# A decoder layer on one core: attention outputs divided on packed rows that DMAs lay, instead of on token rows that TensorE turns

## The chip, the core and the metric

The kernel runs on one core of a Trainium2 chip. The core has TensorE (PE: matrix products and transposes, results in PSUM), VectorE (DVE), ScalarE (ACT), GpSimd (POOL) and SyncE (SP), which here only issues DMAs. Each engine runs its own instructions in order and waits on semaphores for the others. The metric is the device time of one execution in microseconds.

## The reference

A decoder layer in fp32 on 16 sequences of 256 tokens, width 256, 16 heads of 16: causal self-attention, cross-attention to a context, and a mixture of 8 experts with 2 chosen per token, each with a residual and a layer norm.

```python
k, q, v = x @ Wk.T, x @ Wq.T, x @ Wv.T          # per head; k and q normalised per head
att = softmax(where(causal, -inf, q k^T))        # 16 heads, 256 x 256 each
x = layernorm(x + (att @ v) @ Wo.T + bo)
Q, K, V = x @ Wq + bq, ctx @ Wk + bk, ctx @ Wv + bv   # rotary positions on Q and K
x = layernorm(x + (softmax(Q K^T / 4) @ V) @ Wo + bo)
x = layernorm(x + moe(x))                        # top 2 of 8 experts, 256 -> 512 -> 256
```

## The kernel before

Attention runs first, then the experts. Attention is 32 blocks: block n below 16 is the self-attention of sequence n, block n from 16 up the cross-attention of sequence n - 16. A block has 16 heads in 4 groups of 4. The work is a software pipeline of quarters: in quarter q each engine runs the steps whose place in the pipeline falls on it (`q = 4 n + AT`), in an order written out by hand at the end of each engine's part, by r = q mod 4. Each quarter carries the scores of one group (`score`, lines 494 to 510), the maxima of an earlier step's scores (`maxima`, L1075, on VectorE, a first and a second half), the transposed scores (`score_T`, L534), their exponentials (`weights`, L871, ScalarE), and the weighted sum of a group (`weigh`, L555). Four such quarters are one block.

`weigh` multiplies by `vaug`, in which each head has 16 columns of values and 16 columns of ones. So its result for a group, 128 x 256, holds for each of the 4 heads 16 rows of outputs and below them 16 equal rows of the sum of the weights, tokens along the free axis. ScalarE copies it to `oT` (`drain_pv`, L882). What follows for block n:

- quarter r = 2 (`OUT_AT` = 18): TensorE turns `oT` to token rows, four transposes for each half of the tokens (`turn_o`, L655). VectorE inverts the 16 sums per token (L1204, 128 x 16) and multiplies (L1208, 128 x 256), once for each half (`divide`).
- quarter r = 3 (`PROJECT_AT` = 19): TensorE turns the result back (`turn_on`, L669, four transposes) before `weigh`, ScalarE copies it (`drain_onT`, L854), and at the end of the quarter, behind `score_T` and the transposes of the next keys (`turn_qk("k01")`, L645), TensorE multiplies by the output weights (`project_o`, L681). VectorE adds the residual (`residual`, L1219) at the end of its quarter, behind maxima, `combine` (L1082) and `variances` (L1152).

All small results of TensorE (everything but the scores) go through a ring of two PSUM slots. `ring_places` lists the jobs in TensorE's order; a job may start when the one two places before it is drained. `k01` is drained by ScalarE (L920), and the scores of quarter r = 0 wait for that copy.

SyncE issues the DMAs in order. In quarter r = 0: the maxima rows to their place (`lay_max`, L382, four DMAs) and, for 12 of the blocks (n = 2 to 13), two DMAs of 1.5 MB each that fill the experts' row buffer in HBM with padding rows (`lay_pads`, L392; one more of 1.1 MB at n = 2, L395). In r = 1, in self-attention, the next rows of x (`load_xb`, L375); in r = 3 the next transposed inputs (`load_xin`, L367).

## Time and profile before

| | |
|---|---|
| time, median of 3 runs | 1244.41 us (1242.04 to 1250.48) |
| the profiled execution, its own time | 1243.51 us |
| its span in the profile | 1241.8 us |
| TensorE / VectorE / ScalarE / GpSimd busy | 88% / 65% / 46% / 22% |
| mean granted TensorE clock | 0.926 of full speed |
| period of a self-attention block | 22.4 us |
| period of a cross-attention block | 25.6 to 28.6 us at full clock |

Attention takes the first 900 us of the span, the experts the rest. The granted clock is 1.00 (2.4 GHz) or 0.50 (1.2 GHz) at any moment; a number between is a mean over a stretch. In the rows of a stretch an engine's number is its busy time in us. A row of the order of time merges neighbours of one kind; "[1.82 <-PE PS L510]" behind it says that the engine had been idle for 1.82 us until that line of TensorE released it.

### The profile page before, as it was taken

Reading aid. Unit: us, or ns where it says so; the run is one execution under the profiler, and the core shown is the slowest. Engines: PE = TensorE matmul, PEld = TensorE weight load, DVE = VectorE, ACT = ScalarE, POOL = GpSimd, SP = SyncE. Lnnn points to the kernel's source line nnn. Section 1 sums busy time; section 2 is a strip of 40 time slices with the busy share of each in tenths; the row PEclk is TensorE's granted clock in tenths of the full one; section 3 lists DMA queues with packets and bytes.
Section 4 is the critical chain, followed back from the end, with each engine's and each line's share of the span. In section 5 each row is a group of like instructions: output and inputs, shape, how many; then the busy total and the mean of one; then the engine's idle time right before and its main releaser. Section 6 shows DMA issues by size and latency. Waiting matters only on the chain.

```text
span 1241.8 us, 29875 instructions
## 1 busy us (share of the span) xinstructions
PE 1096.5 (88%) x11181; PEld 801.0 (65%) x11181; DVE 801.8 (65%) x1935; ACT 575.2 (46%) x937; POOL 274.3 (22%) x311
## 2 busy tenths in 40 slices
PE   5899999999999899999999999888539999999920
PEld 3456666666666666666666666555439999999920
DVE  5647777778788787687777786753624444444447
ACT  2356666666655555555455554544212222222214
POOL 4022223232222200003030302202132222222210
PEclk9889999999999999999899998876669999999975
DMA  6104644635531000101010100001057767777654
GB/s 229 63 22 160 203 150 143 201 126 183 169 118 29 10 11 19 44 10 48 10 46 11 47 15 33 29 11 38 22 173 209 211 220 213 212 220 214 194 235 188
DMA packets 94651, 139.31 MB, mean 112 GB/s; under 512 B 11216, under 2 KB 68944, under 8 KB 93104
## 3 DMA queue, kind: packets, MB, share of 16 engines
q1 hardware_dynamic: 87888, 114.98, 29.8%
q0 software_dynamic: 6624, 22.42, 4.7%
q8 instruction: 93, 1.52, 0.5%
q14 instruction: 46, 0.38, 0.1%
HBM read 76.56 MB, written 60.29 MB: 110 GB/s over the span
## 4 chain that ended last, share of the span: by engine, by line
PE 75%; DVE 14%; issue 5%; ACT 3%; DMA 2%; POOL 1%; SPq 1%; ACTq 0%; POOLq 0%; DVEq 0%
PE PS L792 10%; PE PS L803 10%; PE PS L534 9%; PE PS L555 8%; PE PS L645 5%; PE PS L503 5%; PE PS L614 4%; PE PS L610 4%; DVE part L1075 3%; PE PS L681 3%; PE PS L628 2%; PE PS L510 2%; PE PS L655 2%; PE PS L669 2%; PE PS L506 2%
## 5 line engine op out<-in xcount | busy, mean ns | idle before, releaser
L1075 DVE TENSOR_REDUCE part<-PS 128x6 f32<-128x768 f32 (+1 forms) x256 | 272.5, 1087 | 114.2 <-PE PS L510 65.2
L871 ACT ACTIVATE pT<-PS 128x768 f32<-128x768 f32 (+1 forms) x256 | 220.8, 914 | 96.7 <-PE PS L534 96.7
L1536 POOL TENSOR_SCALAR_AFFINE_SELECT pT<-pT 128x512 f32<-128x512 f32 x128 | 87.6, 689 | 294.2 <-ACT pT L871 291.2
L534 PE MATMUL PS<-big 17*128 17x256 f32 (+1 forms) x2048 | 142.0, 393 | 9.7 <-DVE part L1075 6.6
L792 PEld LDWEIGHTS PS<-oT,big 128*128 128x128 f32 x1136 | 139.3, 194 | 5.2 <-ACT oT L982 1.6
L555 PE MATMUL PS<-pT,vaug 128*32 128x256 f32 (+1 forms) x2048 | 130.9, 375 | 12.0 <-DVE sq L1178 4.6
L792 PE MATMUL PS<-oT,big 128*128 128x128 f32 x1136 | 139.9, 277 | 1.0 <-ACT oT L982 1.0
L534 PEld LDWEIGHTS PS<-big 17*128 17x128 f32 x2048 | 98.7, 194 | 57.7 <-DVE part L1075 28.2
L803 PE MATMUL PS<-w2s,qkn 128*128 x568 | 134.4, 380 | 0.0
L1553 POOL DMA_INDIRECT xs_dram<-rows_all,posi x64 | 64.3, 1004 | 298.8 <-DVE posi L1331 282.9
L982 ACT ACTIVATE oT<-PS 128x256 f32<-128x256 f32 x71 | 27.2, 383 | 192.5 <-PE PS L781 192.5
L1572 POOL DMA_INDIRECT p_dram<-pT,rowid x71 | 68.1, 959 | 209.7 <-DVE rowid L1433 202.4
L803 PEld LDWEIGHTS PS<-w2s,qkn 128*128 128x128 f32 x568 | 102.4, 190 | 11.3 <-issue 0.3
L555 PEld LDWEIGHTS PS<-pT,vaug 128*32 128x32 f32 x2048 | 57.2, 112 | 60.3 <-issue 35.3
L882 ACT ACTIVATE oT<-PS 128x256 f32<-128x256 f32 x128 | 49.0, 383 | 98.9 <-PE PS L555 98.4
L1417 DVE TENSOR_TENSOR qkn<-PS,b1T 128x512 f32<-128x512 f32 x71 | 49.1, 691 | 65.2 <-PE PS L792 65.2
L645 PE MATMUL PS<-ident,big 128*128 128x128 f32 x512 | 84.5, 289 | 6.7 <-DVE on L1208 4.2
L1427 DVE TENSOR_TENSOR pT<-PS,w_self 128x256 f32<-128x256 f32 x71 | 30.1, 424 | 87.8 <-PE PS L803 87.8
L503 PE MATMUL PS<-big 16*128 16x256 f32 x1024 | 76.3, 413 | 9.4 <-ACT big L916 6.1
L645 PEld LDWEIGHTS PS<-ident,big 128*128 128x128 f32 x512 | 55.0, 143 | 42.7 <-issue 32.3
L614 PE MATMUL PS<-w_self,xin 128*128 128x512 f32 x128 | 68.4, 664 | 1.7 <-DVE w_self L1017 1.3
L503 PEld LDWEIGHTS PS<-big 16*128 16x128 f32 x1024 | 48.0, 190 | 27.4 <-ACT big L916 11.9
(166 smaller groups left out, 1603.6 us busy)
## 6 DMA issues: line engine op xcount, KB each, us to landing
big<-w SPq DMA_DIRECT2D x71, 512.0 KB
xs_dram<-zrow SPq DMA_DIRECT2D x24, 1496.0 KB, 9.0
oT<-xs_dram SPq DMA_DIRECT2D x71, 136.0 KB, 3.5
xin<-xT SPq DMA_DIRECT2D x16, 256.0 KB, 2.8
w2s<-w POOLq DMA_DIRECT2D x1, 4096.0 KB, 12.9
xb<-x SPq DMA_DIRECT2D x16, 256.0 KB, 10.6
xin<-ctxT SPq DMA_DIRECT2D x16, 256.0 KB, 2.8
big<-p_dram SPq DMA_DIRECT2D x4, 1024.0 KB, 7.9
```

Source lines behind the costliest of these rows:

```text
L503: ins = pe.matmul(o, q, a[r0:r0 + D, 1, g, :], start=True, stop=True)
L534: ins = pe.matmul(o, keys, a[r0:r1, 0, g, q0:T], start=True, stop=True)
L555: ins = pe.matmul(o[PADDED * i:PADDED * (i + 1), q0:T], vaug[:, n % 4, kt, GRP * g + i, :], pT[:, k % 2, i, kt * T:kt * T + T - q0], start ...
L614: ins = pe.matmul(o, a[:, c, t * P:(t + 1) * P], w_qk[:, c, :], start=(c == 0), stop=(c == KC - 1))
L645: ins = pe.transpose(ring_slot(job)[:, j * T + t * P:j * T + (t + 1) * P], src, ident[:])
L792: ins = pe.matmul(moe_bank(1, j % 2)[:, f * P:(f + 1) * P], w1s[:, j % W1_BUFFERS, c, f * P:(f + 1) * P], xsT[:, j % 2, c * P:(c + 1) * P] ...
L803: ins = pe.matmul(moe_bank(3, j % 2)[:, 0:E], hact[:, j % 2, c * P:(c + 1) * P], w, start=(c == 0), stop=(c == FC - 1))
L871: act.activation(pT[:, k % 2, 2 * half:2 * half + 2, 0:wide], src, ACT.Exp).then_inc((exp_a, exp_b)[half], 1)
L1075: dve.tensor_reduce(dst, src, AX.X, ALU.max, negate=True).then_inc((max_a, max_b)[half], 1)
L1536: pool.affine_select(d, d, [[0, 2], [0, 2], [1, P]], ALU.is_ge, 0.0, base=0, channel_multiplier=-1).then_inc(masked, 1)
L1553: pool.indirect_dma_start(out=xs_dram, out_offset=bass.IndirectOffsetOnAxis(ap=posi[:, batch_index(last), c:c + 1], axis=0), in_=rows_all[ ...
L1572: pool.indirect_dma_start(out=p_dram, out_offset=bass.IndirectOffsetOnAxis(ap=rowid[:, o, 0:1], axis=0), in_=ye[:, o], in_offset=None).the ...
```

## The change

The two turns on TensorE go, and the copy between them. `oT` is laid on packed rows by SyncE: `packed` has 128 partitions (16 per head, 8 heads in one slice of the free axis and 8 in the other), once for the outputs and once for the sums. 16 DMAs per block move 16 rows x 2 groups x 256 tokens each (32 KB), 8 for groups 0 and 2 in quarter r = 0 (`PACK_AT` = 16), 8 for groups 1 and 3 in quarter r = 1. VectorE inverts all 128 x 512 sums and multiplies 128 x 512 once per block, at the end of quarter r = 2. `project_o` reads `packed` and moves from the end of quarter r = 3 to its start, ahead of `weigh`, so the ring's order there is `wo`, `pv`, `k01`. Per block the change takes away 12 transposes, one copy on ScalarE, and two inversions and two products on VectorE; it adds 16 DMAs, one inversion and one product.

```diff
@@ ring_places, in the order of quarters
-            place("o0", block_at(q, OUT_AT))
-        else:
-            place("onT", block_at(q, PROJECT_AT))
+        elif r == 3:
+            place("wo", block_at(q, PROJECT_AT))
         place("pv", group_at(q, WEIGH_AT))
@@ SyncE
+            def pack(n, b):
+                if n is None:
+                    return
+                if b == 0 and n >= 1:
+                    await_filled(sp, ("wo", n - 1))
+                for g in range(b, NG, 2):
+                    await_drained(sp, ("pv", (n, g)))
+                for k in range(2):
+                    for i in range(GRP):
+                        r0, r1 = PADDED * i + D * k, (GRP * b + i) * D
+                        sp.dma_start(packed[r1:r1 + D, k], oT[r0:r0 + D, n % 2, b::2, :]
+                                     ).then_inc(packed_in[n % 2], 16)
@@
                 load_xb(block_at(q, MAXT_AT + 1))
+                pack(block_at(q, PACK_AT), 0)
+                pack(block_at(q, PACK_AT + 1), 1)
                 n = block_at(q, MAXT_AT)
                 if n is not None:
                     lay_pads(n)
@@ TensorE
             def project_o(n):
-                await_drained(pe, ("onT", n))
+                pe.wait_ge(divided, n + 1)
-                        ins = pe.matmul(ring_slot(job)[:, t * E:(t + 1) * E], onT[:, c, t * P:(t + 1) * P],
+                        ins = pe.matmul(ring_slot(job)[:, t * E:(t + 1) * E], packed[:, 0, c, t * P:(t + 1) * P],
@@
-                    turn_o(block_at(q, OUT_AT), 0)
-                else:
-                    turn_on(block_at(q, PROJECT_AT))
+                elif r == 3:
+                    project_o(block_at(q, PROJECT_AT))
                 weigh(group_at(q, WEIGH_AT))
@@
-                    turn_o(block_at(q, OUT_AT), 1)
@@
                     turn_qk("k01", block_at(q, TURN_K01), 1, 0)
-                    project_o(block_at(q, PROJECT_AT))
@@ ScalarE
-                    await_filled(act, ("o1", n - 2))
+                    act.wait_ge(packed_in[n % 2], 256 * (n // 2))
@@
-                elif r == 3:
-                    drain_onT(block_at(q, PROJECT_AT))
@@ VectorE
+            def divide(n):
+                dve.wait_ge(packed_in[n % 2], 256 * (n // 2 + 1))
+                dve.reciprocal(packed[:, 1], packed[:, 1]).then_inc(inverted, 1)
+                dve.wait_ge(inverted, n + 1)
+                dve.tensor_tensor(packed[:, 0], packed[:, 0], packed[:, 1], ALU.mult).then_inc(divided, 1)
@@
                     maxima(group_at(q, SCORE_AT), 0)
-                    divide(block_at(q, OUT_AT), 0)
                     maxima(group_at(q, SCORE_AT), 1)
                     scale_heads(block_at(q, SCALE_AT))
                     lay_out(block_at(q, LAY_AT))
-                    divide(block_at(q, OUT_AT), 1)
+                    divide(block_at(q, PROJECT_AT - 1))
```

The change moves lines by a few numbers; in the rows below `project_o` is L681 before and L668 of the changed kernel, `score_T` L534 and L545, `weigh` L555 and L566, `turn_qk` L645 and L656. On TensorE, from the scores of a quarter r = 3 to those of the next r = 0 in self-attention, before:

```order
L506 MATMUL PS<-big 128x128 x4
L510 MATMUL PS<-big 128x256 x4
L669 MATMUL PS<-ident,on 128x128 x4
L555 MATMUL PS<-pT,vaug 32x256 x4
L555 MATMUL PS<-pT,vaug 32x128 x4
L534 MATMUL PS<-big 128x256 x4
L534 MATMUL PS<-big 128x128 x4
L645 MATMUL PS<-ident,big 128x128 x4
L681 MATMUL PS<-w_self,onT 128x256 x4
```

And in the changed kernel:

```order
L517 MATMUL PS<-big 128x128 x4
L521 MATMUL PS<-big 128x256 x4
L668 MATMUL PS<-w_self,packed 128x256 x4
L566 MATMUL PS<-pT,vaug 32x256 x4
L566 MATMUL PS<-pT,vaug 32x128 x4
L545 MATMUL PS<-big 128x256 x4
L545 MATMUL PS<-big 128x128 x4
L656 MATMUL PS<-ident,big 128x128 x4
```

The output projection stands where the four transposes stood, and the transposes of the keys are now the last thing before the next scores.

On SyncE, from the maxima rows of one block to the next transposed input, in a block that fills padding, before:

```order
L367 DMA xin<-xT 128x2x256
L382 DMA big<-nmaxT 1x4x256 x4
L392 DMA xs_dram<-zrow 128x11x272 x2
L375 DMA xb<-x 128x2x256
L367 DMA xin<-xT 128x2x256
```

And in the changed kernel (`xin` is L363 there, `nmaxT` L378, `zrow` L401, `xb` L371):

```order
L363 DMA xin<-xT 128x2x256
L378 DMA big<-nmaxT 1x4x256 x4
L391 DMA packed<-oT 16x2x256 x8
L401 DMA xs_dram<-zrow 128x11x272 x2
L371 DMA xb<-x 128x2x256
L391 DMA packed<-oT 16x2x256 x8
L363 DMA xin<-xT 128x2x256
```

The first eight new DMAs stand ahead of the padding, the second eight behind the padding and the rows of x.

## Rows read from the trace of the kernel before

**Rows 1.** The page: busy us by engine and share; a DMA issue, KB, us to landing.

```profile
PE 1096.5 (88%) x11181; PEld 801.0 (65%) x11181; DVE 801.8 (65%) x1935; ACT 575.2 (46%) x937; POOL 274.3 (22%) x311
...
xin<-xT SPq DMA_DIRECT2D x16, 256.0 KB, 2.8
```

**Rows 2.** The chain in order of time, 200 to 260 us: start, us, engine and line.

```profile
221.59 0.59 PE PS L655 x4
...
227.68 0.59 PE PS L669 x4
228.27 0.79 PE PS L555 x16
229.05 0.87 PE PS L534 x16
...
230.50 1.73 PE PS L681 x8
...
232.26 0.30 PE PS L494 x16
```

**Rows 3.** VectorE in order of time, 221 to 233 us: start, us, line, operation.

```profile
221.67 0.96 DVE L1075 TENSOR_REDUCE part<-PS 128x6 f32<-128x768 f32 x1 [1.12 <-PE PS L510]
...
224.03 1.28 DVE L1141 TENSOR_TENSOR big<-qkn,chain 128x512 f32<-128x512 f32 x2
...
227.76 1.82 DVE L1075 TENSOR_REDUCE part<-PS 128x6 f32<-128x768 f32 x2 [1.82 <-PE PS L510]
...
229.80 1.22 DVE L1152 TENSOR_REDUCE vv<-sq 128x64 f32<-128x1024 f32 x1
232.27 0.69 DVE L1219 TENSOR_TENSOR y<-PS,xb 128x512 f32<-128x512 f32 x1 [1.26 <-PE PS L681]
```

**Rows 4.** ScalarE in order of time in the same block.

```profile
217.20 0.38 ACT L882 ACTIVATE oT<-PS 128x256 f32<-128x256 f32 x1
...
229.98 1.51 ACT L871 ACTIVATE pT<-PS 128x768 f32<-128x768 f32 x2 [0.48 <-PE PS L534]
231.38 0.78 ACT L920 ACTIVATE big<-PS,gv 128x512 f32<-128x512 f32 x1
```

**Rows 5.** Groups by line and shape, whole span: busy us, mean ns of one.

```profile
L1204 DVE RECIPROCAL rec<-PS 128x16 f32<-128x16 f32 x64 | 15.9, 248 | 17.8 <-PE PS L655 17.7
...
L1292 DVE RECIPROCAL prob<-odds 128x4 f32<-128x4 f32 x7 | 1.2, 178 | 0.2
```

**Rows 6.** SyncE's DMA issues in order of time, the same block.

```profile
211.62 2.47 SPq L382 DMA_DIRECT2D big<-nmaxT  x4
214.14 1.31 SPq L392 DMA_DIRECT2D xs_dram<-zrow  x2
215.49 3.61 SPq L375 DMA_DIRECT2D xb<-x  x1
226.18 0.38 SPq L367 DMA_DIRECT2D xin<-xT  x1
```

**Rows 7.** DMA issues, 214 to 232 us: KB each, us from issue to landing.

```profile
xb<-x SPq DMA_DIRECT2D x1, 256.0 KB, 11.3
```

**Rows 8.** Stretches: length, busy us of PE, PEld, DVE, ACT, POOL, PEclk, DMA share, GB/s.

```profile
613.70:644.60 30.90, 29.60 (x270) 19.80 (x270) 20.18 (x46) 15.12 (x23) 10.68 (x10) 0.89 0.14 46
...
672.90:700.70 27.80, 26.46 (x270) 18.13 (x270) 20.25 (x46) 15.12 (x23) 10.68 (x10) 1.00 0.15 52
...
426.00:427.00 1.00, 0.00 (x0) 0.00 (x0) 0.93 (x4) 0.57 (x1) 0.00 (x0) 1.00 0.00 0
...
430.00:431.00 1.00, 1.00 (x10) 0.36 (x3) 0.83 (x6) 0.24 (x1) 0.00 (x0) 0.50 0.00 0
```

**Rows 9.** VectorE in a cross-attention block: the pair of maxima of its quarter 3.

```profile
692.59 2.36 DVE L1075 TENSOR_REDUCE part<-PS 128x4 f32<-128x1024 f32 x2 [2.45 <-PE PS L503]
```

**Rows 10.** ScalarE in order of time, the last block, 876 to 882 us.

```profile
876.55 0.38 ACT L882 ACTIVATE oT<-PS 128x256 f32<-128x256 f32 x1 [1.23 <-PE PS L555]
...
881.05 0.60 ACT L854 ACTIVATE onT<-PS 128x512 f32<-128x512 f32 x1 [0.26 <-PE PS L669]
```

## What the change does to the time

> **What bounds the kernel now.** First the page: TensorE is busy for 1096.5 of some 1242 us [rows 1]. Then the chain of waits in order of time: through a self-attention block it runs over TensorE alone, and each group starts where the last one ended [rows 2]. So a microsecond taken off TensorE looks like one won, as long as the other engines have room for it. Two transposing steps of 0.59 us in quarter 2 (one stands in the rows) and one in quarter 3 [rows 2] are 1.77 us per block, 57 us over 32 blocks. Then the order of time on VectorE, ScalarE and SyncE in the same block, which says how much room there is: VectorE waits 1.12 us before quarter 2's maxima and 1.82 us before quarter 3's [rows 3]. ScalarE's copy of `k01` ends at 232.16, and the scores of the next quarter 0 start at 232.26 [rows 2, 4]: that copy is as late as it may be, and only because the 1.73 us of output projection lie between it and the scores.
>
> **The inversion.** It is the dearest new operation and no row shows its size. 128 x 4 takes 178 ns, 128 x 16 takes 248 ns [rows 5]: 5.8 ns per element and partition, where a product of 128 x 512 takes 0.69 us in all [rows 3]. At 5.8 ns, 508 further elements come to 2.96 us, so I take 3.14 us. The lower bound is the 0.69 us of the product. The upper bound scales the larger row, fixed part and all: 32 x 0.248 = 7.9 us; the two rows speak against that, since four times the elements cost 1.4 times as much.
>
> The Trainium skill (VectorE: DVE Perf Modes, First, the fixed hardware budget) says that the inversion is an iterative divide with a repeat count of 8. At 8 cycles of that page's kind per element, 0.96 GHz as Trainium Kernel Development and Optimization of the Trainium skill (NeuronCore Architecture) has it, it would be some 4.3 us, an estimate; the trace's 5.8 ns per element lies below it. By that estimate the sum below would be some 35 us larger.
>
> **A block whose DMAs come in time.** I walk one self-attention block, with the times of the rows as they stand.
> - VectorE, quarter 2: the first maxima start at 221.67 as before, the pair takes 1.82, `scale_heads` 1.28 [rows 3]: 224.8. Inversion and product 3.83: 228.65. Before, the two small inversions and products took 1.34 together.
> - TensorE does not gain quarter 2 in full. Without the first turn `weigh` ends at 222.4, but `score_T` waits for the first maxima (222.63 at the earliest), so 0.2 of 0.59 us is won there. The second 0.59 counts in full. The scores of quarter 3 end at about 226.8 instead of 227.68 (before, quarter 3's first transposes began there [rows 2]).
> - `project_o` is next and waits for the product: 228.65, 1.9 us idle. It takes 1.73, `weigh` 0.79, `score_T` 0.87 [rows 2]: 232.1. Behind the waiting projection stand all three, and the exponentials wait for them.
> - `k01` needs the ring slot of `wo`, which `residual` drains. VectorE does its pair of maxima (1.82, from 228.65), `combine` (0.17, about what a short operation takes), `variances` (1.22) and `residual` (0.69) [rows 3]: 232.6. So `k01` runs to 233.2.
> - ScalarE's exponentials end at 232.1 + 0.1 + 1.51 = 233.7, its copy of `k01` at 234.5 [rows 4]. The cover (the projection) is gone: the scores start at 234.55 instead of 232.26 [rows 2].
>
> That is +2.3 us per block instead of -1.77. Are the DMAs in time? Group 3 is copied at 217.20 + 0.38 [rows 4]. A DMA with the same number of dimensions takes SyncE 0.38 us, 0.41 with its gap; one of `lay_max` takes 0.61 [rows 6]; eight take 3.3 (bounds 3.0 to 4.9). Landing is 2.8 us after issue for `xin` [rows 1], so all is there at about 223.4, before 224.8. Hidden, with 1.4 us to spare; at 0.61 each it is just hidden.
>
> **Blocks with padding.** Here they are not in time. The two fills are issued at 214.14; the issue of `xb` behind them takes 3.61 us instead of the 0.38 of its like [rows 6], so the queue is full, and `xb` lands 11.3 us after it started, at 226.8 [rows 7]. The second eight DMAs stand behind both. The first eight stand ahead of the fills and wait for group 2's copy, so they push the fills back by 3.3 us: `xb` lands at 230.1, and the last packed rows, 256 KB more on the same queue, at about 230.7. VectorE is ready at 224.8: it waits 5.9 us, and everything of the walk above moves by that. +8.2 us per block. These are blocks 1 to 12 (the pack of block m shares a quarter with the fill of m + 1), 12 x 8.2 = 98 us; the third fill at n = 2 adds its 1.1 MB, at the rate of the others (3.25 MB in some 11 us) 3.5 us. Lower bound: if the queue did not hold them, 2.3 each.
>
> The Trainium skill (DMA: Bandwidth & Descriptors, Queues, rings and completion order) speaks against this change: each DMA engine takes the descriptors of one issuer's queue in ring order. The long issue of `xb` in the trace agrees with it. By that rule the padded blocks cost the 98 us; without it they would cost 28.
>
> **The clock.** TensorE would stand idle from 226.8 to about 234.6 in such a block. In the trace it stood idle through 426 to 427, and at 430 the granted clock was 0.50, that is 1.2 GHz [rows 8]. A block in which the clock fell took 30.9 us, a like one at full clock 27.8 [rows 8]: 3.1 us. 12 blocks x 3.1 = 37 us. Lower bound 0 (it doesn't fall), upper bound twice that (it stays low for twice as long).
>
> **The rest.** Blocks 0, 13, 14 and 15 have no fill beside them: 4 x 2.3 = 9 us. In cross-attention VectorE idled 2.45 us before quarter 3's pair [rows 9], and what it gets more there is 3.83 - 1.34 = 2.5 us, so that pair starts where it did. The logits' product still lies between `k01` and the next scores, so no cover is lost. What remains is `k01` waiting for the residual: 0.5 us by the same walk, and some 1.5 in every second block, where the router's choice stands behind the division. 14 x 1.0 = 14 us; bounds -1 and +2.5 per block. At the end nothing hides the DMAs: in the last block group 3 is copied at 876.93 and the projection could start at 881.65 [rows 10]. Now 3.3 + 2.4 for issue and landing and 3.83 on VectorE: 886.5, 4.8 later; 3 more in the block before. 8 us.
>
> **Sum.** 98 + 3.5 + 37 + 9 + 14 + 8 = 169.5 us on the profiled execution's own 1243.5 us: 1413 us. That execution is 0.9 us under the median of the runs, so nothing is added.
>
> **Rivals.**
> - *The queue does not hold the packed rows* (they land as in other blocks, and the clock stays). 12 x 2.3 instead of 12 x 11.3 + 3.5: 1413 - 112 = 1301. For it: only two DMA types are seen behind a fill, and one of them has no late user. Against: 11.3 us for 256 KB.
> - *The inversion is cheap* (0.69 us, the lower bound). 2.45 us less in 12 blocks, 1.9 in 4 and some 1.5 in 14, where other waits take over: 58 us less, 1355. Against it: the slope in rows 5.
> - *All of it dearer*: inversion half as long again (4.7 us), or the clock low for twice as long, or falling in cross-attention too, where a fall cost 3.1 us: 1413 + some 60 = 1475.
> - *Faster: TensorE's sum decides.* If the divided rows lay ready when quarter 3's scores end, nothing of the walk waited for the projection, and 57 us of transposes went: 1187. It decides from the point where inversion and product together take less than 226.8 - 224.8 = 2.0 us and the rows have landed by 224.8, in padded blocks too. Even then the copy of `k01` has lost its cover. 3 in 100.
> - *No change*: the gain in some blocks balances the stall in others, which takes a cheap inversion and early landing both. 3 in 100.
>
> **Numbers.** The forecast has 52 in 100 (its own range 1365 to 1455), the dearer case 18, the queue that doesn't hold 15, the cheap inversion 9, no change 3, faster 3. The range 1300 to 1490 leaves out some of the dearer case and of the first rival, and the last two. A measurement of this kernel can tell about 1% from no change. Slower by over 1%: 0.94, within 1%: 0.03, faster by over 1%: 0.03.
>
> **What would show it.** In the changed profile: one inversion of 128 x 512 per block with its mean (3.1 us right; 0.7 or 4.7 wrong). Idle time of VectorE before it, released by the DMAs, about 6 us in 12 blocks and none in the others. Idle time of TensorE before the projection. Block periods of about 34 us up to 500 us of the span, then 24 to 29. A clock below 1.00 in self-attention. Idle of TensorE before quarter 0's scores, released by ScalarE's copy of `k01`. It would be wrong if the packed rows landed early beside the fills, or if the issue of one took much more than 0.4 us: at 1 us each even the free blocks would wait.

## The result, and the profile after

The changed kernel takes 1509.15 us (median of 4 runs, 1504.82 to 1512.9) against 1243.22 us of the kernel before on the same chip: ratio 1.212, interval 1.208 to 1.216. The forecast was 1413 us, in a range of 1300 to 1490. The direction was right, and the loss is half as large again as forecast: 269 us between the two profiled executions instead of 169.5.

| | before | after |
|---|---|---|
| span in the profile, us | 1241.8 | 1511.1 |
| TensorE busy, us | 1096.5 | 1170.1 |
| VectorE busy, us | 801.8 | 878.9 |
| mean granted TensorE clock | 0.926 | 0.819 |
| one of the 12 blocks with padding, maxima rows to maxima rows, us | 22.4 to 24.5 | 36.9 to 41.3 |
| a cross-attention block, us | 25.6 to 31.5 | 29.6 to 35.8 |

TensorE has 12 transposes per block less and is busy for longer, because the same products run at the lower clock. First the page: an engine's busy time; then the costliest groups (busy us, mean ns of one, idle time before them and its releaser) and the DMA issues (KB each, median us to landing).

```profile
PE 1170.1 (77%) x10797; PEld 822.1 (54%) x10797; DVE 878.9 (58%) x1871; ACT 555.0 (37%) x905; POOL 269.0 (18%) x311
...
L1173 DVE RECIPROCAL packed<-packed 128x512 f32<-128x512 f32 x32 | 107.2, 3349 | 117.9 <-DMA packed<-oT 117.9
...
packed<-oT SPq DMA_DIRECT2D x512, 32.0 KB, 2.0
```

The inversion takes 3.35 us, and VectorE stood idle for 117.9 us ahead of it, always for the packed rows. Next the waits of TensorE: total, times, longest.

```profile
PE PS L668 <- DVE packed L1175: 146.4, 28, 11.5
PE PS L505 <- ACT big L893: 24.4, 14, 1.8
PE PS L514 <- ACT big L889: 20.3, 26, 2.0
```

The projection (L668) waits for the division, and the scores (L505 in self-attention, L514 in cross-attention) for ScalarE's copy of `k01`: the two waits of the walk. A block with padding in order of time: SyncE's issues, then VectorE, TensorE and ScalarE. They answer to [rows 6], [rows 3], [rows 2] and [rows 4].

```profile
259.37 2.55 SPq L378 DMA_DIRECT2D big<-nmaxT  x4
262.03 5.16 SPq L391 DMA_DIRECT2D packed<-oT  x8
267.23 1.39 SPq L401 DMA_DIRECT2D xs_dram<-zrow  x2
268.67 4.27 SPq L371 DMA_DIRECT2D xb<-x  x1
273.04 8.00 SPq L391 DMA_DIRECT2D packed<-oT  x8
...
282.44 3.35 DVE L1173 RECIPROCAL packed<-packed 128x512 f32<-128x512 f32 x1 [6.55 <-DMA packed<-oT]
285.82 0.69 DVE L1175 TENSOR_TENSOR packed<-packed 128x512 f32<-128x512 f32 x1
...
286.57 3.78 PE L668 MATMUL PS<-w_self,packed 128*128 128x256 f32 x8 [8.43 <-DVE packed L1175]
...
294.54 0.40 PE L505 MATMUL PS<-identb,strips 32*128 32x64 bf16 x16 [1.76 <-ACT big L893]
...
293.66 0.78 ACT L893 ACTIVATE big<-PS,gv 128x512 f32<-128x512 f32 x1
```

Eight packing DMAs take SyncE 5.16 us, 0.64 each, and the eight behind `xb` 8.00 us. VectorE gets the rows 23.07 us after the first DMA of the maxima rows (259.37 to 282.44); over the 12 blocks with padding it is 23.2 us on the mean, 26.1 in the one with the third fill and 22.4 to 23.7 in the others. The landings of `xb`, of the first packing DMA behind it and of the last two:

```profile
xb<-x SPq DMA_DIRECT2D x1, 256.0 KB, 11.3
...
packed<-oT SPq DMA_DIRECT2D x1, 32.0 KB, 5.8
...
packed<-oT SPq DMA_DIRECT2D x2, 32.0 KB, 2.0
```

The first one behind the padding takes 5.8 us from its issue to its landing. The last one takes 2.0, as the median of all 512 does, so the packed rows are complete 2.0 us after SyncE has begun the last issue: the padding delays them by holding up SyncE's issues. TensorE is then idle for 8.43 us, does the projection in 3.78 us instead of 1.73, and waits 1.76 us more for `k01`. Last, the stretches of attention (length, busy us of PE, PEld, DVE, ACT and POOL, clock, DMA share, GB/s): all of it and then the last 16 blocks, of after.

```profile
0.00:1102.40 1102.40, 866.95 (x8716) 548.80 (x8719) 689.43 (x1299) 447.95 (x702) 176.15 (x215) 0.81 0.26 75
...
593.60:1102.40 508.80, 445.50 (x4047) 290.67 (x4048) 372.82 (x750) 224.94 (x350) 68.28 (x66) 0.85 0.15 38
```

And of before, for the same blocks:

```profile
0.00:848.00 848.00, 793.33 (x9073) 525.15 (x9073) 617.88 (x1359) 466.99 (x732) 181.40 (x215) 0.96 0.24 78
...
394.30:848.00 453.70, 424.85 (x4235) 287.16 (x4233) 332.05 (x782) 235.69 (x366) 68.40 (x66) 0.95 0.08 24
```

Attention, up to the last maxima rows, grew by 254 us. TensorE's idle time in it went from 54.7 to 235.5 us: +181. Its busy time went up by 73.6 although 57 us of transposes are gone, so 130 us are the same work at the lower clock. 181 - 57 + 130 = 254. In the last 16 blocks it is +34 us of idle time, -28 of transposes, +49 of clock: +55.

### The profile page after: what moved, and what is told of

It reads as the page before. It is cut to its first block, busy times and chain, and to the rows that moved or that the text cites. A ratio compares the mean times of both kernels' runs of the same rounds, so it can differ in the third digit from the quotient of the medians.

```text
span 1511.1 us, 29429 instructions
## 1 busy us (share of the span) xinstructions
PE 1170.1 (77%) x10797; PEld 822.1 (54%) x10797; DVE 878.9 (58%) x1871; ACT 555.0 (37%) x905; POOL 269.0 (18%) x311
## 4 chain that ended last, share of the span: by engine, by line
PE 60%; DVE 17%; SPq 8%; issue 5%; ACT 5%; DMA 3%; POOL 1%; ACTq 0%; POOLq 0%; DVEq 0%
PE PS L775 9%; PE PS L786 8%; PE PS L545 8%; PE PS L566 7%; SPq L391 6%; DVE packed L1173 6%; PE PS L668 6%; PE PS L625 4%; PE PS L621 4%; PE PS L514 4%; DVE part L1046 3%; ACT pT L844 2%; PE PS L656 2%; DMA packed<-oT 2%; PE PS L521 2%
## 5 line engine op out<-in xcount | busy, mean ns | idle before, releaser
L1173 DVE RECIPROCAL packed<-packed 128x512 f32<-128x512 f32 x32 | 107.2, 3349 | 117.9 <-DMA packed<-oT 117.9
L545 PE MATMUL PS<-big 17*128 17x256 f32 (+1 forms) x2048 | 156.8, 427 | 20.1 <-DVE part L1046 18.8
L1501 POOL TENSOR_SCALAR_AFFINE_SELECT pT<-pT 128x512 f32<-128x512 f32 x128 | 81.8, 640 | 506.4 <-ACT pT L844 502.4
L566 PE MATMUL PS<-pT,vaug 128*32 128x256 f32 (+1 forms) x2048 | 155.0, 430 | 8.6 <-issue 5.3
L668 PE MATMUL PS<-w_self,packed 128*128 128x256 f32 x128 | 54.9, 603 | 125.8 <-DVE packed L1175 125.8
L545 PEld LDWEIGHTS PS<-big 17*128 17x128 f32 x2048 | 108.0, 215 | 79.6 <-issue 40.0
L668 PEld LDWEIGHTS PS<-w_self,packed 128*128 128x128 f32 x128 | 37.0, 303 | 139.7 <-DVE packed L1175 132.2
L566 PEld LDWEIGHTS PS<-pT,vaug 128*32 128x32 f32 x2048 | 62.0, 125 | 87.1 <-issue 64.7
L514 PE MATMUL PS<-big 16*128 16x256 f32 x1024 | 83.4, 444 | 23.1 <-ACT big L889 20.3
L656 PE MATMUL PS<-ident,big 128*128 128x128 f32 x512 | 84.2, 289 | 9.9 <-DVE y L1185 6.1
L625 PE MATMUL PS<-w_self,xin 128*128 128x512 f32 x128 | 84.9, 803 | 1.7 <-DVE w_self L988 1.3
```

Source lines behind the costliest of these rows:

```text
L514: ins = pe.matmul(o, q, a[r0:r0 + D, 1, g, :], start=True, stop=True)
L545: ins = pe.matmul(o, keys, a[r0:r1, 0, g, q0:T], start=True, stop=True)
L566: ins = pe.matmul(o[PADDED * i:PADDED * (i + 1), q0:T], vaug[:, n % 4, kt, GRP * g + i, :], pT[:, k % 2, i, kt * T:kt * T + T - q0], start ...
L625: ins = pe.matmul(o, a[:, c, t * P:(t + 1) * P], w_qk[:, c, :], start=(c == 0), stop=(c == KC - 1))
L656: ins = pe.transpose(ring_slot(job)[:, j * T + t * P:j * T + (t + 1) * P], src, ident[:])
L668: ins = pe.matmul(ring_slot(job)[:, t * E:(t + 1) * E], packed[:, 0, c, t * P:(t + 1) * P], w[:, c, :], start=(c == 0), stop=(c == KC - 1))
```

## Experiments

Ratios are to the kernel before on the same chip, with their 95% intervals. Unless said otherwise the edit is made to the changed kernel, which gave 1.211 again:

> The changed kernel itself once more, so that the runs beside it are compared on one chip. Every theory expects its ratio to the kernel before of 1.21 again.

Measured: 1.2111 (1.2069 to 1.2152).

Four runs need care: `pads_later`, `busy_wait`, `cheap_inverse` and `wo_last` ran on a chip on which the kernel before took 1269 us (1260 to 1277), 2% more than the 1240 to 1246 elsewhere, and the changed kernel did not run there. The intervals don't cover that. So their gains over the changed kernel are given twice, by the difference of the ratios and by that of the medians; which of the two is nearer is not known.

A second caution: the last 16 blocks (maxima rows to maxima rows) are the same program in the changed kernel, in `busy_self` and in `pads_later`. They took 508.5, 492.8 and 526.4 us, at clocks of 0.86, 0.89 and 0.84. The last two:

```profile
567.56:1060.35 492.79, 432.56 (x4056) 283.12 (x4059) 371.86 (x751) 224.68 (x349) 68.75 (x66) 0.89 0.15 39
...
508.12:1034.50 526.38, 455.12 (x4048) 296.47 (x4051) 373.49 (x751) 224.32 (x349) 66.94 (x66) 0.84 0.14 37
```

So kernels that differ only in the first half of attention differ by 16 to 18 us in the second, and the clock with it; what sets it there is not shown. A gain of that size is placed only by looking at the blocks themselves.

**The DMAs alone.** The kernel before, with `pack(...)` at its two places and no reader.

```diff
+                pack(block_at(q, OUT_AT - 2), 0)
+                pack(block_at(q, OUT_AT - 1), 1)
```

> The kernel before, unchanged in what it computes, with the 16 packing DMAs of each block added at the places that they have in the changed kernel; nothing reads the packed rows, and only the reuse of oT two blocks later waits for them. My theory: the DMAs cost through whoever waits for them and not by themselves. In a fill block xb then lands some 20.5 us after the first DMA of the maxima rows, which is 232.1 on the times of the kernel before, where the residual wants it at 232.3: ratio 1.000 to 1.010. Rival: the transfers or their issue disturb the rest (xin and xb late on SyncE's queue, traffic to SBUF): 1.03 or more, which would be a part of the 21% that does not come from the wait for the division.

Measured: 1.0074 (1.0031 to 1.0118). So 512 further DMAs cost under 1% by themselves. But SyncE has no room left in a block with padding:

```profile
193.23 2.55 SPq L384 DMA_DIRECT2D big<-nmaxT  x4
195.89 5.16 SPq L397 DMA_DIRECT2D packed<-oT  x8
201.09 1.40 SPq L407 DMA_DIRECT2D xs_dram<-zrow  x2
202.54 4.83 SPq L377 DMA_DIRECT2D xb<-x  x1
207.47 7.57 SPq L397 DMA_DIRECT2D packed<-oT  x8
215.09 0.58 SPq L369 DMA_DIRECT2D xin<-xT  x1
215.72 2.55 SPq L384 DMA_DIRECT2D big<-nmaxT  x4
```

From one block's maxima rows to the next (22.5 us) it issues without a pause. What costs is who waits for these DMAs.

**Padding behind the packed rows.**

```diff
-                n = block_at(q, MAXT_AT)
+                n = block_at(q, MAXT_AT + 1)
                 if n is not None:
                     lay_pads(n)
```

> The changed kernel with the two padding fills issued behind the second eight packing DMAs instead of ahead of them; nothing else moves. Queue theory: in the 12 blocks with a fill the packed rows land some 2 us after their last issue, VectorE's wait before the inversion (117.9 us in the changed kernel) falls below 20 us, and since TensorE's idle stretch of about 8 us there shrinks to about 2, the clock recovers too: 12 x (6.5 + some 5 us of half clock) = 140 us less, some 1370 us. Rival (the DMAs are late from their own 16 issues of 0.6 us, not from the fills): the wait stays and the time stays within 20 us of 1509.

Measured: 1.137 (1.128 to 1.146), 93 us less by the ratios and 63 by the medians, and not the 140 expected. The 12 blocks with padding take 371 us instead of 454, 29.7 to 31.7 each and one 34.0. VectorE's wait for the rows in them fell from 91 to 21 us. In six of them the rows are still late by 2.4 to 3.7 us, in the other six by under 0.5. One of the first six:

```profile
258.64 5.55 SPq L391 DMA_DIRECT2D packed<-oT  x8
264.24 0.58 SPq L371 DMA_DIRECT2D xb<-x  x1
264.94 6.08 SPq L391 DMA_DIRECT2D packed<-oT  x8
...
272.48 3.35 DVE L1174 RECIPROCAL packed<-packed 128x512 f32<-128x512 f32 x1 [3.45 <-DMA packed<-oT]
```

The maxima rows start at 255.96, VectorE is ready 13.1 us later, as the walk had it (224.8 - 211.6), and the rows are there after 16.5. In the walk they were there after 11.8. SyncE's last issue ends 15.1 us after the maxima rows started, where the block of the changed kernel above has 21.7: the 6.6 us between them are the whole difference of the landings (16.5 for 23.1).

**The first eight from GpSimd's queue.** In the changed kernel (`after_pool`), and with the padding and the projection moved as well (`pool_queue`).

```diff
-                pack(block_at(q, PACK_AT), 0)
...
+                        pool.dma_start(packed[r1:r1 + D, k], oT[r0:r0 + D, n % 2, 0::2, :]
+                                       ).then_inc(packed_lo[n % 2], 16)
```

> The changed kernel with one edit: GpSimd issues the first eight packing DMAs of each block, so that the padding on SyncE's queue starts 5.2 us sooner. If issue time ahead of the padding adds to the landing of the second eight one for one, they land 17.9 us after the first DMA of the maxima rows instead of 23.1, and VectorE waits 1.3 us instead of 6.5 in 12 blocks: 62 us less, ratio 1.16. Rival: the landing is set by the transfers of the padding and the first eight now share the engines with it, so the wait stays: 1.20 to 1.22.

Measured: 1.1714 (1.1672 to 1.1756), nearer to 1.16 than to the rival. But over the 12 blocks VectorE gets the rows 3.6 us earlier on the mean (19.6 us after the maxima rows, for 23.2), not 5.2, and waits 2.9 us for them, not 1.3. In one of the latest (249.82 to 270.59, 20.8 us) its wait is 4.38 us: the second eight, queued behind `xb`, took 8.25 us to issue as before, and start no earlier than group 3's copy allows. Issue ahead of the padding adds to the landing, but not one for one.

> Padding later and projection last, and the first eight packing DMAs of each block are issued by GpSimd instead of SyncE. My theory says that the issue time on SyncE (0.64 us each) sets when the rows land: the second eight can start when group 3 is copied, some 3.5 us earlier than in the run without this edit, where VectorE waited 3.84 us for them in a fill block. 12 x 3.5 us less: ratio 1.063. Rival: the rows land when the transfers allow it, or GpSimd issues no faster and its masks come late: 1.09 to 1.12.

Measured: 1.0576 (1.0495 to 1.0656), where the same kernel with SyncE's queue alone has 1.097 (`later_last`, below). The wait ahead of the inversion fell from 3.84 to 0.91 us:

```profile
269.61 3.35 DVE L1174 RECIPROCAL packed<-packed 128x512 f32<-128x512 f32 x1 [0.91 <-DMA packed<-oT]
```

**The inversion.** A maximum of the same shape in its place; the output is then multiplied by the sums and not divided.

```diff
-                dve.reciprocal(packed[:, 1], packed[:, 1]).then_inc(inverted, 1)
+                dve.tensor_tensor(packed[:, 1], packed[:, 1], packed[:, 1], ALU.max).then_inc(inverted, 1)
```

> The changed kernel with a maximum of the sums with themselves (128 x 512, same operands) in place of the inversion, so outputs are multiplied by the sums, not divided. It prices the inversion, 3.35 us each in the profile, against 0.69. Theory that each inversion stands on the path (TensorE waits for the product in 28 of 32 blocks): 2.66 x 28 = 74 us less and, with shorter idle stretches of TensorE, some more from the clock: 1400 to 1435 us. Rival (in cross-attention the order of the quarter's end sets the time, and beside the fills the clock stays low): 40 us less or under that, 1470 or more.

Measured: 1.1565 (1.1468 to 1.1663): 68 us less by the ratios, 52 by the medians. The rows' lateness stays: VectorE still idles 123.5 us for them.

**The projection back at the quarter's end.** Ring order `pv`, `k01`, `wo`.

```diff
-                elif r == 3:
-                    project_o(block_at(q, PROJECT_AT))
...
                     turn_qk("k01", block_at(q, TURN_K01), 1, 0)
+                    project_o(block_at(q, PROJECT_AT))
```

> The changed kernel with the output projection back at the end of quarter 3, behind the transposes of the next keys, and the ring's order pv, k01, wo as in the kernel before. Cover theory: the scores of quarter 0 no longer wait for ScalarE's copy of the keys (24.4 and 20.3 us on TensorE in the changed kernel) nor the keys for the residual, and the 1.9 us wait ahead of the projection is partly filled with the weighted sum: 1.0 to 1.6 us per block, 35 to 60 us less with the clock, 1450 to 1475 us. Rival (VectorE's division holds the maxima and so score_T whatever stands first): within 15 us of 1509.

Measured: 1.1617 (1.154 to 1.1695), 61 us less by the ratios, 36 by the medians. `k01` has its cover again; the wait went to `score_T`, whose maxima stand behind the inversion on VectorE:

```profile
PE PS L544 <- DVE part L1044: 196.1, 58, 15.4
```

With the padding later too:

> Both single moves together: fills behind the packing DMAs, and the output projection last in quarter 3. If the two costs are independent, 6% and 4% of the kernel before come off: a ratio of about 1.09 to before. If both are the same wait seen twice, about 1.13. Neither theory expects it to reach 1.00, since the inversion (3.35 us) still stands on the path.

Measured: 1.0973 (1.0893 to 1.1052). By the ratios the two gains add up (0.075 + 0.050 of 0.212 leave 0.087, measured 0.097), by the medians they more than do (63 + 36 us, measured 143 on one chip with `after_again`). That both are the same wait seen twice (1.13) is ruled out either way. With the cheap operation in the inversion's place as well:

> Padding later and projection last, as in the run before (1.097), and the inversion of 128 x 512 replaced by a maximum of the same shape, so the output is multiplied by the sums and not divided. It leaves open what keeps this layout above the kernel before. If every block still waits for the inversion, 31 x 2.66 us go: ratio 1.031. If other waits take over in part, as they did when the same edit was made to the changed kernel alone (68 us won instead of 82): 1.043. If TensorE's shorter list decided once the inversion is cheap: 0.96 to 1.00.

Measured: 1.0408 (1.0332 to 1.0485): other waits take over in part. And with GpSimd's queue besides:

> Padding later, projection last, first eight packing DMAs from GpSimd (1.058), and a maximum in place of the inversion, so the output is multiplied by the sums and not divided. It asks whether anything but the inversion keeps this layout above the kernel before once the rows land in time. 2.66 us in 31 blocks would be 82 us, ratio 0.99; by the share that the same edit won with SyncE's queue (1.097 to 1.041, 70 us): 1.00. If other waits take over: 1.02 to 1.04.

Measured: 0.9922 (0.9889 to 0.9956). This is the one kernel that ends below the one before, by 0.8%, and it leaves the inversion out. Its self-attention blocks from the third on take 21.5 to 22.3 us where those of before take 22.4, and the last two 23.1 and 22.7 for 24.4 and 24.1, all at clock 1.00. So the gain that TensorE's list promised (1.77 us per block) exists, by half, once the division is cheap and its rows are in time.

**TensorE's clock.** Products of 128 x 512 that nobody reads, ahead of the wait for the division, keep TensorE busy and leave the other engines alone.

```diff
+                for _ in range(16 if 1 <= n <= 12 else 3 if n < B else 1):
+                    pe.matmul(ring_slot(job), wx_q[:, 0, 0:P], wx_q[:].rearrange("p c e -> p (c e)"),
+                              start=True, stop=True)
                 pe.wait_ge(divided, n + 1)
```

> The changed kernel with matmuls that nobody reads on TensorE (512 columns, fp32) right ahead of the wait for the divided rows: 16 in the blocks beside a fill, 3 in the other self-attention blocks, 1 in cross-attention. They write the ring slot that the projection then overwrites. Clock theory: the wait itself stays, but the granted clock (0.72 over a block beside a fill) comes back to near 1.00 and such a block falls from 37.9 us to about 31: 12 x 6 to 7 = 75 us less, and some more in the blocks behind: 1400 to 1440 us. Rival (the period is set by VectorE and the DMAs, and the low clock lies in their shadow): no change, or up to 20 us slower by the added matmuls.

Measured: 1.2292 (1.2204 to 1.2379), slower by 21 us by the ratios and 52 by the medians, a miss of the experiment: the 16 products took 14.0 us, 0.875 each, and ran 2 us past the division in the block shown. In most others they held TensorE for longer (blocks of 40.0 to 44.3 us beside this one's 37.5).

```profile
281.93 14.00 PE L665 MATMUL PS<-wx_q 128*128 128x512 f32 x32
```

It still shows one thing: at the full clock, too, the rows land 23.09 us after the maxima rows started (266.68 to 289.77), against 23.07 at a clock of 0.80, and 23.5 against 23.2 on the mean of the 12 blocks. The landing does not hang on the clock. With 8 products, and none in cross-attention:

> The changed kernel with idle-filling matmuls only as long as the wait: 8 (0.87 us each) in the blocks beside a fill, 2 in the other self-attention blocks, none in cross-attention. Theory from the run with 16: beside a fill the period is set by the DMAs up to the landing (23.1 us after the maxima rows' first DMA, at either clock), so only the part behind it gains from the clock, 14.9 us against 12.4: 12 x 2.5 = 30 us less than the changed kernel. Rival (clock theory of the prediction's successor: the whole loss of 7 us per block comes back): 75 us less.

Measured: 1.1845 (1.1758 to 1.1933), 31 us less by the medians, as expected in total but not in place. In the profiled execution, 42 us shorter than that of `after_again`, the 12 blocks with padding took 22 us less (432 for 454, 1.8 each) and the last 16 blocks, to which nothing was added, 17 us less. With one product ahead of each of the two waits in cross-attention, none elsewhere:

> The changed kernel with one such matmul in cross-attention ahead of the wait for the divided rows, and one ahead of the scores' wait for ScalarE's copy of the keys; self-attention untouched. Theory that a cross-attention block takes 31.7 us on the mean instead of 29.7 because the clock falls in more of them: the clock stays up and some 2 us x 14 = 28 us come back. Rival (its 3.5 us over before are waits on VectorE and on the copy alone): no gain, or a few us slower.

Measured: 1.2098 (1.2044 to 1.2152), nothing gained beyond the intervals. In the profiled execution the last 16 blocks took 8 us less (500.4 for 508.5), which is no more than they differ by without an edit; the clock over them rose from 0.86 to 0.90 only.

**The division behind the maxima of quarter 3**, on the kernel with padding later and projection last.

```diff
-                    divide(block_at(q, PROJECT_AT - 1))
                     choose_second(block_at(q, SECOND_AT))
...
                     maxima(group_at(q, SCORE_AT), 1)
+                    divide(block_at(q, PROJECT_AT))
```

> Padding later and projection last, and on VectorE the inversion and the product stand behind the pair of maxima of quarter 3 instead of ahead of it. In the fill blocks of the run without this edit, TensorE waited 5.8 us at score_T for maxima that were queued behind the inversion. My theory: with the maxima ahead, only the projection at the quarter's end waits. By the times of that run: maxima to 266.4, inversion and product to 270.5, projection to 272.2, and the next scores at 272.3 instead of 276.3. 4.0 us less in 12 fill blocks, some 2 in the 18 others: 84 us of the 121 over the kernel before go, ratio 1.03; at half of it in the others 1.045. Rival: the wait only moves from score_T to the projection and to the copy of k01: 1.09.

Measured: 1.1484 (1.1411 to 1.1559): slower, against both expectations. In self-attention it helped (blocks of 27.3 us instead of 27.3 to 30.7). In cross-attention TensorE has one wait of 3.38 us for the division in each of twelve blocks, where the kernel without the edit waited at `score_T` for up to 2.4 us. Seven of the twelve grew to 37.3 to 38.1 us, the other five take 30.9 to 34.4. Stretches behind that wait, first in cross-attention, then in self-attention:

```profile
692.20:700.00 7.80, 7.79 (x35) 6.17 (x36) 2.38 (x5) 0.00 (x0) 1.26 (x1) 0.50 0.02 9
700.00:707.00 7.00, 7.00 (x42) 4.16 (x41) 4.11 (x12) 3.29 (x5) 0.00 (x0) 0.50 0.10 21
707.00:717.00 10.00, 9.58 (x100) 5.97 (x98) 6.99 (x21) 4.49 (x8) 0.00 (x0) 0.95 0.19 38
...
266.60:271.00 4.40, 4.38 (x32) 3.19 (x36) 1.74 (x3) 0.00 (x0) 0.00 (x0) 0.50 1.06 330
271.00:280.00 9.00, 8.81 (x128) 5.18 (x125) 7.87 (x20) 4.86 (x9) 1.27 (x2) 1.00 0.13 29
```

After 3.4 us of idling in cross-attention TensorE runs at 1.2 GHz for 14.8 us without a pause; after 3.53 us in self-attention for 4.4 us. Four products that nobody reads in the place of the wait, in cross-attention alone:

> The kernel with the division behind quarter 3's maxima (1.148), and in cross-attention alone four products of 128 x 512 that nobody reads stand on TensorE ahead of its wait for the divided rows, 0.875 us each and so as long as the wait (3.4 us). They leave the work and the waits of every other engine as they are. If the granted clock, at half for some 15 us behind that wait, is what makes a block 37.6 us long, cross blocks fall to some 31 us, 6 us less in the 11 blocks that were slow and 1 to 2 in the others: 70 us, ratio 1.09. If the blocks were long because the wait itself pushes the other engines, nothing changes: 1.15.

Measured: 1.1008 (1.0963 to 1.1053). The slow cross blocks went from 37.6 to 31 us, the twelve from 35.7 to 30.3 on the mean, those of self-attention stayed at 27.3. The filled wait is as long as the idle one was. So through the clock a wait of 3.4 us cost 6.6 us more than the wait itself in the slow blocks, 5.4 on the mean.

**More time for the division.** The projection one quarter later, `k01` ahead of `weigh`, the division behind quarter 3's maxima and `combine`.

```diff
-PACK_AT, PROJECT_AT, LN_AT = 16, 19, 21
+PACK_AT, PROJECT_AT, LN_AT = 16, 20, 21
```

> Correct division again, rows packed by GpSimd (first eight) and SyncE, padding later. New: the output projection stands one quarter later (quarter 0 of the next block, behind score_T), the inversion and the product stand in VectorE's quarter 3 behind the maxima and combine, the residual in its quarter 0, and the transposes of k01 and their copy stand ahead of weigh in quarter 3. By the walk: VectorE's pair ends 1.8 us after quarter 3's scores, the product 4.2 later, at 6.1; TensorE asks for it after k01, weigh, score_T, the next scores, the turned maxima, weigh and score_T, at some 6.3. If that holds, no engine waits for the division and TensorE's shorter list decides: some 1.5 us less per block than before, ratio 0.96 to 0.98. Rival: VectorE, 4 us later at quarter 0's maxima, holds score_T there, and the clock falls: 1.03 or more.

> The same with all 16 packing DMAs on SyncE's queue. With a quarter more of time the issue on one queue should be hidden too: same as nq_pool within 1%. Rival: the issue (6 us for eight behind the maxima rows, and the wait for the projection that frees the packed rows) still makes them late: 3% or more above nq_pool.

Measured: 1.1313 (1.1271 to 1.1355) and 1.1288 (1.1254 to 1.1321). The queue no longer matters, as the second text says. The rival of the first one holds: `score_T` of a quarter waits for the maxima of the same quarter, and those stand behind the division.

```profile
260.48 0.94 PE L546 MATMUL PS<-big 17*128 17x256 f32 x16 [2.93 <-DVE part L1049]
```

Some cross blocks take 42 us in turn with others of 29 there. The long ones have a clock of 0.74 and the short ones one of 0.97:

```profile
674.96:717.47 42.51, 32.87 (x266) 22.03 (x267) 30.02 (x65) 14.92 (x23) 7.45 (x11) 0.74 0.11 26
717.47:746.80 29.33, 25.61 (x257) 16.96 (x255) 20.69 (x40) 14.55 (x22) 11.81 (x15) 0.97 0.21 58
```

No run with added products separates the clock from the waits there.

**In two halves** of 128 x 256, on the kernel with GpSimd's queue: one in quarter 2, one behind quarter 3's maxima.

```diff
-                    divide(block_at(q, PROJECT_AT - 1))
+                    divide(block_at(q, PROJECT_AT - 1), 0)
...
+                    divide(block_at(q, PROJECT_AT), 1)
                     combine(block_at(q, MAXT_AT - 1))
```

> Correct division, padding later, projection last in its quarter, first eight packing DMAs from GpSimd (1.058), and one edit: inversion and product are cut in two halves of 128 x 256 (some 2.1 us each), one at the end of VectorE's quarter 2, where it idles 2.3 us, the other behind the maxima of quarter 3. The theory that the loss is the 4 us that VectorE spends in one piece between TensorE's asking and its going on: score_T of quarter 3 then finds its maxima (54.9 us of waits on it go), and the projection waits some 0.7 us for the second half. 0.98 to 1.01. Rival: two short waits lower the clock as one long one did, or the halves cost more than half: 1.04 to 1.06.

Measured: 1.0643 (1.0586 to 1.0701), no gain over 1.0576. Half of the theory holds: a block with padding takes 23.1 to 25.1 us, 1.3 less on the mean. The stretch from 600 to 900 us lost it again, at a clock of 0.86 against 0.89. That the clock is the reason was not tested in this kernel.

## Why the prediction was right in its sign and wrong in its size

- **Right: TensorE's sum does not decide.** The projection waits for the division (146.4 us), `k01` lost its cover (24.4 and 20.3 us), and moving the projection back won 36 to 61 us.
- **Right: the padding on SyncE's queue holds the packed rows.** With the padding behind them the 12 blocks took 82 us less. The Trainium skill (DMA: Bandwidth & Descriptors, Queues, rings and completion order) says that each DMA engine takes a queue's descriptors in ring order. The trace agrees: the first packing DMA behind the padding needed 5.8 us to land, the last 2.0. But what delays the last rows is SyncE's issue: it comes later by 6.6 us, as much as the landing.
- **Right within 0.2 us: the inversion**, 3.35 us for 3.14. The rival at half as long again, and the 4.3 us estimated from the Trainium skill (VectorE: DVE Perf Modes, First, the fixed hardware budget), are too high; the measurement decides.
- **Near: the cost of the low clock in a padded block, 3.1 us in the forecast.** From the landing to the next maxima rows the 12 blocks take 14.6 us on the mean, and the forecast has the same with those 3.1 us in it (22.4 + 8.2 + 3.1 - 19.1). In `busy_self` it is 12.8 on the mean, and 11.9 in five blocks, one of which had a clock of 0.99 there. So 1.8 us came back and 2.7 are the most that the clock can have cost: 22 to 32 us in the 12 blocks, for 37.
- **Wrong: the landing in padded blocks, the step "at about 230.7" (19.1 us after the maxima rows).** Measured 23.1. It took 0.41 us of issue for each packing DMA, by `xin`'s row; it is 0.64, nearer to the 0.61 of `lay_max` that stood beside it in [rows 6]: 1.85 us for the first eight, by which `xb` lands later (20.6 us after the maxima rows, for 18.5). The forecast let the last rows land 0.6 us behind `xb`, at the rate of the transfers. The eight behind `xb` take 8.0 us to issue instead of 3.3; the last is begun when `xb` has landed and needs 2.0 us itself, so they land 2.4 us behind `xb`. 4.0 us x 12 = 48 us in blocks like the one shown. What follows the landing took as long as forecast, and one of the 12 blocks took 2 us longer in the kernel before too (24.4 for 22.4). The 12 blocks cost 183 us instead of 138.5.
- **Wrong: "Hidden, with 1.4 us to spare".** The walk let the second eight start when group 3 is copied. They stand behind the first eight and `xb`, which at 0.41 us each would have been out by then; at 0.64 they start 9.0 us after the maxima rows, not 6.0, and with 6.1 us of issue they land after 16.5 us instead of 11.8. So the rows are late by up to 3.7 us in half of the blocks even with the padding out of their way, as the run with the padding behind them shows, and the text's "at 0.61 each it is just hidden" left the first eight out. In the changed kernel itself it showed in one free block only, the first after the padding (34.7 us for 24.1), where VectorE waited 5.31 us; there four further loads stood on the queue between the two eights, 2.77 us of issue. In two others (31.2 us for 26.1, 30.9 for 25.8) it did not wait for the rows.
- **Wrong: the cross-attention term of 1.0 us.** Blocks 15 to 30 cost 55 us, 3.4 each (the first two stand in the forecast as free blocks, at 2.3 us each). VectorE never waited for the packed rows there. The waits alone do not exceed the term: 34 us more idle time of TensorE less 28 us of transposes is 6 us, 0.4 in a block, and a block with a clock of 0.96 took 29.6 us for 28.3. The rest, 49 us, is the clock, which the forecast let fall in padded blocks only: by so much TensorE's busy time is above what the removed transposes leave. That one wait can cost about twice its length on top of itself in this stretch was shown on another kernel (`divide_q3`, `divide_q3_busy`). In the changed kernel itself two added products won nothing clear, so which of its short waits lower the clock stays open. The forecast had this as part of its "dearer" rival, at 18 in 100 and priced at 60 us, with the issue cost left out of it.
- **Wrong in size: the end.** 15 us instead of 8. The last two divisions wait 22.1 us in sum for their rows.

The misses sum up: 45 in the padded blocks, 55 in the rest (5 + 10.6 + 55 + 15 measured for 31), 100 us in all. The range was too narrow at its upper end for two reasons. The bound of 0.61 us per DMA, which the text names, was taken only for the free block and not carried into the padded ones (8 x 0.2 us x 12 = 19 us for the first eight alone). And the low clock in cross-attention stood in a rival, not in the sum.

## What to carry to other kernels

Taking instructions off the busiest engine wins nothing if their replacement has a longer way from the last input to the result: compare the time from ready to needed, not the sums. Price a DMA's issue by the row nearest in shape, count all of them one after another on their queue, and check whether the queue's period is already full. A wait of TensorE costs more than its length where the stretch behind it then runs at half clock, and an edit in one stretch can change the clock of another, so compare block by block before a small gain is put down to the edit. Cutting a 4 us piece of another engine or moving it a quarter only helps if the next reader is not the same engine's older work.

## What the runs showed of the hardware that was not expected

- Inversion on VectorE: 128 x 16 in 248 ns, 128 x 256 in 1746 (`two_halves`), 128 x 512 in 3349. That is 6.25 ns per element of the free axis beyond the first 16.
- Issuing a DMA of 16 partitions from SBUF to SBUF (32 KB) takes SyncE 0.64 us, 0.81 to 1.05 on the mean of eight when they follow `xb` behind the padding (12 blocks of the changed kernel), and GpSimd 0.56 us (eight in 4.45, `pool_queue`). It lands 2.0 us after its issue has begun.
- 512 such DMAs added to the kernel before, in which TensorE is busy for 88% of the span, cost 0.7% (`before_dmas`).
- The same 3.4 to 3.5 us of idling was followed by 14.8 us at half clock in cross-attention, TensorE busy all through it, and by 4.4 us in self-attention (`divide_q3`).
- The last 16 blocks, the same program in three kernels, took 492.8, 508.5 and 526.4 us at mean clocks of 0.89, 0.86 and 0.84.
